# A bias addition moved from GpSimd to VectorE, and VectorE's order in the last stage of a two-layer graph network

## What is computed

```python
h = relu(layernorm(x))
# layer 0: attention over the edges, then a feed-forward part
q, k, v = split(layernorm(h, ga, ba) @ Wqkv + bqkv)      # 8 heads of 32
agg = segment_sum(softmax_over_dst(q[src] . k[dst] * SCALE) * v[src], dst)
y = h + agg
x = x + (y + gelu(layernorm(y, gr, br) @ W_in + b_in) @ W_out + b_out)
# layer 1: messages by one of 8 relations, summed over the edges
h = relu(layernorm(x))
rel = segment_sum((h @ W[r])[src, edge_type], dst)
z = gelu(rel + h @ loop_w + h_bias + h)
x = x + layernorm(z) * gamma + beta
```

## Time and profile before

| what | us |
|---|---|
| three runs | 1413.2, 1415.9, 1416.3; median 1415.9 |
| the profiled execution, its time | 1415.1 |
| its span in the trace (first to last instruction) | 1413.4 |
| PE busy | 1154.9 (82%) |
| GpSimd busy | 995.6 (70%) |
| VectorE busy | 895.7 (63%) |
| ScalarE busy | 453.0 (32%) |

### The profile page before, as it was taken

The page is one execution under the profiler, slowest core; times in us unless marked ns, Lnnn a source line. Parts: engine busy times, 40 slices in busy tenths (PEclk is TensorE's granted clock), DMA queues, the critical chain, the costliest instruction groups (busy, mean ns, idle before and its releaser), DMA issues.

```text
span 1413.4 us, 18069 instructions
## 1 busy us (share of the span) xinstructions
PE 1154.9 (82%) x5223; PEld 829.5 (59%) x5223; DVE 895.7 (63%) x2778; ACT 453.0 (32%) x1150; POOL 995.6 (70%) x1032
## 2 busy tenths in 40 slices
PE   4875859999999999999999989677676767767674
PEld 2443647777777777777777765345454444444453
DVE  5664668888888888888888863124543454345345
ACT  4644215444544454445444533100000000000000
POOL 2755778788878877888788610577777777777773
PEclk9988979999999999999999999777878787788877
DMA  7758787888788878887888621344444444444442
GB/s 245 209 164 297 241 230 208 251 270 262 234 249 264 262 236 241 255 250 227 238 256 252 195 75 60 113 117 127 130 127 133 124 134 124 134 126 128 130 125 86
DMA packets 143355, 266.14 MB, mean 188 GB/s; under 512 B 41674, under 2 KB 89908, under 8 KB 140310
## 3 DMA queue, kind: packets, MB, share of 16 engines
q0 software_dynamic: 59536, 167.31, 41.5%
q1 hardware_dynamic: 82758, 96.47, 20.8%
q10 hardware_dynamic: 960, 1.18, 0.3%
HBM read 199.25 MB, written 65.63 MB: 187 GB/s over the span
## 4 chain that ended last, share of the span: by engine, by line
PE 33%; POOL 26%; DVE 18%; issue 11%; DMA 3%; ACT 0%; POOLq 0%; DVEq 0%; SPq 0%
POOL arena L1279 23%; PE ps L1520 8%; PE ps L1543 6%; PE ps L1551 6%; PE ps L1569 4%; DVE arena L1811 3%; PE ps L1509 3%; DVE arena L1809 3%; DVE arena L1744 2%; POOL arena L1225 2%; PE ps L1681 2%; DMA arena<-h_all,typs 1%; DVE arena L671 1%; PE ps L1489 1%; DVE arena L673 1%
## 5 line engine op out<-in xcount | busy, mean ns | idle before, releaser
L1225 POOL DMA_INDIRECT arena<-qv_tab,srcs x392 | 407.5, 1040 | 127.4 <-issue 115.9
L1279 POOL DMA_INDIRECT arena<-h_all,typs x392 | 381.7, 974 | 159.8 <-issue 117.3
L1681 PE MATMUL ps<-arena 128*128 128x256 f32 x784 | 279.6, 494 | 150.5 <-DMA arena<-h_all,typs 147.1
L1681 PEld LDWEIGHTS ps<-arena 128*128 128x128 f32 x784 | 169.4, 236 | 240.2 <-DMA arena<-h_all,typs 199.5
L1520 PE MATMUL ps<-arena 128*128 128x264 f32 x784 | 213.9, 401 | 30.6 <-DVE arena L1744 30.5
L1569 PE MATMUL ps<-wrel,arena 128*128 128x512 f32 x400 | 189.7, 600 | 2.4 <-ACT arena L1344 2.4
L1520 PEld LDWEIGHTS ps<-arena 128*128 128x128 f32 x784 | 139.1, 193 | 69.1 <-DVE arena L1744 43.9
L1744 DVE TENSOR_TENSOR arena<-arena 128x512 f32<-128x512 f32 x196 | 136.9, 699 | 40.8 <-ACT arena L1312 40.8
L1509 PE MATMUL ps<-arena 128*128 128x264 bf16 x1032 | 142.3, 279 | 11.2 <-DMA arena<-k_tab 11.2
L1509 PEld LDWEIGHTS ps<-arena 128*128 128x128 bf16 x1032 | 125.3, 144 | 44.6 <-issue 35.4
L1869 DVE TENSOR_TENSOR arena<-ps,rowb 128x256 f32<-128x256 f32 x25 | 10.6, 425 | 218.8 <-PE ps L1669 218.8
(11 more groups left out here) (164 smaller groups left out, 1474.6 us busy)
## 6 DMA issues: line engine op xcount, KB each, us to landing
h_all<-arena SPq DMA_DIRECT2D x23, 1024.0 KB, 5.5
arena<-dst SPq DMA_DIRECT2D x49, 256.0 KB, 5.1
rel<-arena SPq DMA_DIRECT2D x77, 128.0 KB, 2.2
arena<-k_tab SPq DMA_DIRECT2D x49, 198.0 KB, 4.1
att<-arena POOLq DMA_DIRECT2D x49, 132.0 KB
qv_tab<-arena SPq DMA_DIRECT2D x25, 256.0 KB, 3.1
arena<-qv_tab,srcs POOLq DMA_INDIRECT x392, 4.2
arena<-h_all,typs POOLq DMA_INDIRECT x392, 2.8
```

Source lines behind the costliest of these rows:

```text
L1225: pool.indirect_dma_start(out=rowbuf[:, 2 * q + t % 2, 0:2 * D], out_offset=None, in_=qv_tab, in_offset=bass.IndirectOffsetOnAxis(ap=srcs[ ...
L1279: pool.indirect_dma_start(out=rows1[:, u * T + t, :], out_offset=None, in_=h_all[0:N * R, :], in_offset=bass.IndirectOffsetOnAxis(ap=typs[ ...
L1681: last = nc.tensor.matmul(ps[:, 6 + u, 0:D], ind1[:, u, t, :], rows1[:, u * T + t, :], start=(t == 0), stop=(v == 0 and t == T - 1))
```

## The change

b_out is loaded into `rowb` in the first stage behind the pieces of x, with a semaphore of its own (`bias_in`). VectorE waits for it ahead of its block loop and adds the row to each block of xs behind that block's take. GpSimd's residual has one addition, no longer two with a semaphore between. `s_w2` counts nine transfers. In the last stage VectorE makes the indicators of visit 0 ahead of the loop. At v it first does loop_sum and combine of the block that ended in the visit before, then copy_h1 and indicators of visit v + 1, and only then finish. h1c has two halves and the loop part two PSUM banks (1 and 2), so that the copy for the next block needn't wait.

```diff
@@ first stage, SP
                 load_x(5)
+                sp.dma_start(rowb[:, 0, :], b_out.partition_broadcast(P)).then_inc(bias_in, 16)
...
-                    if 19 <= b < 23:
-                        sp.dma_start(rowb[:, b - 19, :], (b_out, h_bias, gamma, beta)[b - 19].partition_broadcast(P)).then_inc(s_w2, 16)
+                    if 19 <= b < 22:
+                        sp.dma_start(rowb[:, b - 18, :], (h_bias, gamma, beta)[b - 19].partition_broadcast(P)).then_inc(s_w2, 16)
@@ first stage, VectorE
                 dve.wait_ge(s_w, 64)
+                dve.wait_ge(bias_in, 16)
                 for b in range(NBLK):
...
                     take(b)
+                    nc.vector.tensor_tensor(x_block(xs, b), x_block(xs, b), rowb[:, 0, :], ALU.add)
@@ middle stage, GpSimd
                     pool.wait_ge(x1_ready, m + 1)
-                    nc.gpsimd.tensor_tensor(x_of(m), x_of(m), h_of(m), ALU.add).then_inc(x_added, 1)
-                    pool.wait_ge(x_added, m + 1)
-                    nc.gpsimd.tensor_tensor(x_of(m), x_of(m), rowb[:, 0, :], ALU.add).then_inc(x_ready, 1)
+                    nc.gpsimd.tensor_tensor(x_of(m), x_of(m), h_of(m), ALU.add).then_inc(x_ready, 1)
@@ last stage, buffers, PE
-            h1c = cut([D])
+            h1c = cut([2, D])
...
-                        last = nc.tensor.matmul(ps[0:P, 1, 0:D], h1T1[:, k, :], wloop[:, k, :],
+                        last = nc.tensor.matmul(ps[0:P, 1 + nth(m) % 2, 0:D], h1T1[:, k, :], wloop[:, k, :],
@@ last stage, VectorE
+                indicators(0)
                 for v in range(G):
-                    m = block_of(v)
+                    ended = block_of(v - 1) if v else None
+                    if ended is not None:
+                        loop_sum(ended)
+                        combine(ended)
                     if v - 1 in EARLY:
                         loop_sum(EARLY[v - 1])
-                    if m is not None:
-                        copy_h1(m)
-                    indicators(v)
-                    if v % 2 and v > FIRST:
-                        loop_sum(block_of(v - 1))
-                        if v in EARLY:
-                            copy_h1(EARLY[v])
-                        combine(block_of(v - 1))
-                        finish(block_of(v - 1))
+                    if v + 1 < G:
+                        if loop_of(v + 1) is not None:
+                            copy_h1(loop_of(v + 1))
+                        indicators(v + 1)
+                    if ended is not None:
+                        finish(ended)
```

More of the change, by code:

```diff
@@ L204, in program @@
             kh_ready, r1_ready, km_ready, kl_ready = (sem(n) for n in ("kh_ready", "r1_ready", "km_ready", "kl_ready"))
-            sq_ready = sem("sq_ready")
+            sq_ready, bias_in = sem("sq_ready"), sem("bias_in")
             stored = [sem(f"tables_stored{j}") for j in range(NST)]
@@ L737, in program @@
             sums_in = [sem(f"sums_in{n}") for n in range(2)]
-            x1_ready, x_added, x_ready = sem("x1_ready"), sem("x_added"), sem("x_ready")
+            x1_ready, x_ready = sem("x1_ready"), sem("x_ready")
             yn_ready, y_turned, yT_ready = sem("yn_ready"), sem("y_turned"), sem("yT_ready")
@@ L1253, in residual @@
                     if m == 0:
-                        pool.wait_ge(s_w2, 16 * 10)
+                        pool.wait_ge(s_w2, 16 * 9)
                     pool.wait_ge(x1_ready, m + 1)
-                    nc.gpsimd.tensor_tensor(x_of(m), x_of(m), h_of(m), ALU.add).then_inc(x_added, 1)
-                    pool.wait_ge(x_added, m + 1)
-                    nc.gpsimd.tensor_tensor(x_of(m), x_of(m), rowb[:, 0, :], ALU.add).then_inc(x_ready, 1)
+                    nc.gpsimd.tensor_tensor(x_of(m), x_of(m), h_of(m), ALU.add).then_inc(x_ready, 1)
                 for v in range(G):
@@ L1371, in _ @@
                     if v == FIRST:
-                        act.wait_ge(s_w2, 16 * 10)
+                        act.wait_ge(s_w2, 16 * 9)
                     if v == 0:
@@ L1588, in _ @@
                     if v == FIRST:
-                        pe.wait_ge(s_w2, 16 * 10)
+                        pe.wait_ge(s_w2, 16 * 9)
                     if v + 1 < BY_PE:
@@ L1662, in turn @@
                     for k in range(2):
-                        nc.tensor.transpose(ps[:, 0, k * P:k * P + P], h1c[:, k * 128:k * 128 + 128],
+                        nc.tensor.transpose(ps[:, 0, k * P:k * P + P], h1c[:, nth(m) % 2, k * 128:k * 128 + 128],
                                             ident[0:P, 0:P]).then_inc(h1t_psum, 1)
@@ L1863, in copy_h1 @@
                     dve.wait_ge(h1_kept, m + 1)
-                    nc.vector.tensor_copy(h1c, hs[:, m * D:(m + 1) * D]).then_inc(h1c_ready, 1)
+                    nc.vector.tensor_copy(h1c[:, nth(m) % 2, :], hs[:, m * D:(m + 1) * D]).then_inc(h1c_ready, 1)
                 def loop_sum(m):
@@ L1868, in loop_sum @@
                     dve.wait_ge(loop_psum, nth(m) + 1)
-                    own.did(nc.vector.tensor_tensor(h_m, ps[0:P, 1, 0:D], rowb[:, 1, :], ALU.add))
+                    own.did(nc.vector.tensor_tensor(h_m, ps[0:P, 1 + nth(m) % 2, 0:D], rowb[:, 1, :], ALU.add))
                     own.did(nc.vector.tensor_tensor(xs[:, m * D:(m + 1) * D], xs[:, m * D:(m + 1) * D], rowb[:, 3, :], ALU.add))
                     own.wait()
-                    own.did(nc.vector.tensor_tensor(h_m, h_m, h1c, ALU.add))
+                    own.did(nc.vector.tensor_tensor(h_m, h_m, h1c[:, nth(m) % 2, :], ALU.add))
                     own.wait()
```

## The result

| | before | after |
|---|---|---|
| runs | 1413.2, 1415.9, 1416.3, 1418.8 | 1441.0, 1440.3, 1441.3, 1443.4 |
| median | 1416.1 | 1441.1 |
| profiled execution: time, span | 1415.1, 1413.4 | 1441.0, 1439.3 |
| first gather of the middle stage starts (L1225; after: L1228) | 128.7 | 143.6 |
| from there to the first gather of the last stage | 762.7 | 772.6 |

The ratio is 1.018, 95% interval 1.0156 to 1.0203. The sum said +11.5 and the medians say +25.0. The spans of the two traces differ by 25.9: **+14.9 in the first stage** (I had +12.0), **+9.9 in the middle stage** (I had 0), +1.1 in the last (I had -0.5). Lines of the changed kernel are the old numbers plus one to three; GpSimd's remaining addition is L1259, VectorE's new one L614.

What follows compares the result with a forecast made beforehand. It took PE and VectorE to bound the first and middle stages, GpSimd's gathers the last. 8.1 + 0.7 + 3.2 + 0 - 0.5 = +11.5 on 1415.1 gave 1426.6 us; range 1415 to 1436.

Steps and rivals of the forecast that it cites:

- The additions, +8.1: First stage: VectorE's 25 new additions cost +8.1 us, bounds 5.4 and 12.5; each 0.56 beside GpSimd's work, 0.34 outside.
- The 16 places: First stage: 16 of the 25 additions lie on the critical path; the other nine fall in VectorE's waits for PE.
- The wait, +0.7: Start of the first stage: VectorE's wait for b_out before take(0) costs between 0 and 2 us, taken as 0.7.
- PE's clock, +3.2: First stage: longer gaps put two more projections at PE's slow clock level, +3.2 us; bounds 0 to 10.
- Rival D: First stage: the slow clock level comes after every gap, adding 10 us or more: 1435 and over; chance 9%.
- GpSimd with one addition less, 0: Middle stage: 27 us of work leaves GpSimd, which only waits longer for PE, so the time changes by 0.
- rival B: Middle stage: VectorE's L1809, relieved of GpSimd's second addition, saves 9.7 us, giving 1417; chance 8%.
- The last stage, -0.5: Last stage: VectorE's indicators ahead of finish let the last matmuls start earlier; gain between 1.3 and -0.6 us, taken as -0.5.
- my two cases: End of the last stage: PE's last four matmuls take 1.13 us or, at the slow level, 2.08; end 1395.2 or 1396.2.
- Rival E: Last stage's collisions fall by 4 us, the tail gives 1.3, additions take their low bound: 1416 or less; chance 6%.
- the cycle stays at 28.3: Sign for the middle stage: the cycle of two visits keeps its 28.3 us.
- 12 us together on PE's waits: Sign for the first stage: PE's waits for L524 and L383 grow by some 12 us together.

Runs made afterwards that it cites:

- e8: Changed kernel with VectorE's addition only at the nine visits costed at nothing, b_out left out for the other 16 blocks: 1428.6 us, first stage 131.5.
- e2: Changed kernel without VectorE's 25 additions, its wait for the bias kept: 1425.8 us; first stage 130.3, middle 773.0.
- e3: Kernel before with the last stage's part of the change alone: 1417.0 us, ratio 0.9980 to 1.0004.
- e5: Changed kernel with VectorE's 25 additions moved, five at a time, into its longest wait of each chunk: 1428.2 us, first stage 132.4.
- f1: Kernel before, unchanged, as a control on another chip: 1522.6 us, first stage 127.8, middle 803.1.
- e7: Kernel before without GpSimd's relation weights (set to zero): 1413.4 us, first stage 128.2.
- e1: Changed kernel with GpSimd's second addition made again, so b_out is added twice: 1435.1 us; first stage 145.0, middle 762.7.
- e4: Changed kernel with GpSimd's remaining addition half a visit later: 1432.2 us, middle stage 761.6.
- e6: Changed kernel without GpSimd's relation weights (set to zero): 1440.6 us, first stage 142.7.
- e12: Kernel before, second addition on VectorE in the middle stage, GpSimd's remaining one half a visit later, matmuls filling PE's first-stage gaps: 1510.4 us (before: 1523.3).

## Why the prediction was wrong

The sign was right, the size half. By its steps:

1. *The additions, +8.1.* The 16 places were right (e8), and so was the low bound of the price: the median is 415 ns, an occupancy of 0.34, 5.4 us in all. The 0.56 that I took for collisions was wrong in the first stage (median undisturbed). What one costs there with its consequences is 0.76. The collisions that came were hardly on the additions but on L495 beside them in the queue, which the additions shifted beside GpSimd's instructions: +3.0 us, a term that I didn't have.
2. *The wait, +0.7.* 0 to 1.2 (e2 against e3 and e5), within the bounds.
3. *PE's clock, +3.2.* Mis-sized: 6.3 by the busy time of the projections (84.6 against 78.3 us), 4 to 6 by the matmuls that fill the gaps, in both kernels. I counted two more slow projections, and there were four. The bound of 10 was right. Rival D's time, 1435 and over, was nearer than the forecast, but by luck: its first stage was to be 18.8 us longer and the rest as before, and here 10 of the 25 us come from the middle stage. A higher count could have been had from the earlier trace rows: a gap of 2.09 us was already followed by the slow level, and each chunk has two gaps that the change lengthens. A gap alone doesn't settle the level, though: after 2.15 or 2.16 us, projection 12 took 2.85 us in the kernel before and 4.13, 4.23 and 4.50 in e3, f1 and e7, and in the changed kernel the one at 62.86 stayed at 2.75 after 2.68.
4. *GpSimd with one addition less, 0.* **This step failed.** I asked only whether GpSimd ends the cycle, and priced the removal at nothing since it waits for PE. The wait grew as I said, and L1809's SBUF form fell from 1130 to 684 ns as rival B said. But an engine that gets earlier within its cycle meets another partner. The addition that stayed moved 1.2 us forward beside the weigh that PE waits for: 0.34 on that instruction, 0.43 on the cycle, 23 cycles, +9.9 (e1, e2, e4). I had the price of such a collision in hand (0.44) and used it only for what was removed. The rule on shared interfaces that the prediction cites from the Trainium skill ("GPSIMD Engine Reference", Key points) speaks against the change here: the weigh has two SBUF inputs, and its row shows 1.02 us beside GpSimd and 0.68 alone. I applied it to the collisions that end, not to those that begin. L495 in the first stage is the same omission a second time.
5. *The last stage, -0.5.* +1.1 in this pair of traces: the last matmuls became dependent on the gather as I described, and ran at the slow level, the worse of my two cases. In e1, e4 and e6 the better one came, with a tail of 21.3. Both cases of the sum were real; which one comes was open.

Rival E's time, 1416 or less, doesn't follow from its terms: with the forecast's clock term left in they give 1419. It changes nothing here. The signs that I named beforehand divide likewise. GpSimd's wait, L1809's form, the 392 gathers at 500 us and the end of the wait for L1859 came as told; "the cycle stays at 28.3" and "12 us together on PE's waits" (7.3) did not.

## What to carry to other kernels

When work is taken off an engine that isn't the bound, don't stop at "it waits longer": find where in the cycle its remaining instructions land, and what stands beside them there. Where two engines disturb each other a cycle depends on phase: here a loss of 0.7% came from one instruction's place and went by placing it by hand, and on another chip the same stage had the other sign, for a reason left open. And an instruction in a ring of waits cost more than its own time: the lengthened gaps cost clock on the matrix engine, and a neighbour in the queue was shifted beside another engine's work. Put it in a wait that exists.

## What I had not expected of the hardware

- Additional matmuls that nobody reads shortened a stage: 17 of them took 7.4 us off the changed kernel's first stage and those of e12 3.2 off the old one's.
- One of VectorE's smallest instructions, L495 with 128x5 elements, takes 0.17 us where GpSimd has nothing beside it, but beside GpSimd's two-input instruction it stayed until that one ended, here in both places to within 0.03 us:
```profile
59.69 0.53 DVE L495 TENSOR_SCALAR rsb<-mvb 128x5 f32<-128x5 f32 x1
...
82.10 0.53 DVE L495 TENSOR_SCALAR rsb<-mvb 128x5 f32<-128x5 f32 x1
```
```profile
59.53 0.67 POOL L343 TENSOR_TENSOR arena<-arena 128x256 bf16<-128x256 f32 x1
...
81.94 0.67 POOL L343 TENSOR_TENSOR arena<-arena 128x256 bf16<-128x256 f32 x1
```
  In the changed kernel's trace the longest one, 1.11 us at 45.11, ends 0.03 us behind GpSimd's L334 (1.26 us at 44.93). So in these rows the cost of a collision went by the other engine's instruction, not by the own one's size. It isn't so for every pair: beside GpSimd's L330, which has one tensor as input (1.56 us at 69.05), L495 took 0.54 at 69.22 and ended 0.85 us ahead of it. e6 has it too (0.59 and 0.60 us), since `split_keys` stays there.
- The same program took 1416, 1510 and 1523 us on three chips. On the chip of 1523 us its first stage was that of the first chip within 1 us (127.8 and 128.7); the difference lay in the middle stage (762.7 against 803.1) and the last (522 against 596).
